# A decoder on one Trainium2 core: in cross attention, every third key tile is weighed as three bf16 products in place of one fp32 product

## Chip, cores and metric

The program runs on one core of a Trainium2 chip. The metric is the device time of one execution in microseconds (us); the median of several executions is given. The engines are TensorE (PE in the profile, with PEld for its weight loads), VectorE (DVE), ScalarE (ACT), GpSimd (POOL) and the DMA queues, here issued by SyncE (SP). Each engine works through its own list of instructions in order, and the engines meet only through semaphores.

## What is computed

Two decoder layers on x of shape (4, 256, 256) with a context of (4, 1601, 256). The part that the change touches is the cross attention of the second layer, for 16 query heads over 4 key/value heads of 128 channels:

```
q = rope(rms_norm(x @ Wq.T))            # (4, 16, 256, 128)
kv_in = concat([context, x], axis=1)    # 1601 + 256 = 1857 keys a batch row
k = rope(rms_norm(kv_in @ Wk.T));  v = kv_in @ Wv.T      # 4 heads, each used by 4 query heads
scores = q @ k.T / sqrt(128)
attn = softmax(scores) @ v
x = x + attn @ Wo.T
```

Everything is fp32 in the reference.

## The kernel before

The stages run one behind another: self attention, attention to the context as a memory, a ternary feed-forward, a gated scan, this cross attention, and the experts. The cross attention is `cross_stream` (L1385 on), by far the longest: its steps alone run from 704.0 to 1877.6 us.

**Groups, steps, slots.** A group g is one batch row with one key head: 16 groups (`GROUPS`). The 1857 keys of a group make `KT` = 15 tiles of 128 (the last has 65 rows), the 4 x 256 query columns make two halves of 512. So a group has `STEPS` = 30 steps: step j of a group is key tile t = j // 2 and half n = j % 2; a step counted through the whole stage is s = 30 g + j. The code of every engine is written as a loop over slots; in slot s each engine does its share for step s and whatever else is set down for that slot.

**One step.** `score` (PE, L1585) makes the scores as three bf16 products of high and low halves, 128 keys x 512 columns, in banks 0 and 1. `lower` (DVE, L1793) adds the column's negative bound and writes `lowered`, a ring of three. `exponent` (ACT, L1656) writes p into `p32`, a ring of four. `weigh` (PE, L1598) multiplies values by p in fp32 into bank 2 + n, over all 15 tiles; PE does it two slots late (`BEHIND` = 2). `accumulate` (POOL, L1733) adds p into `acc` for the sum of the softmax.

**Work for the next group in the same slots.** A unit (6 a group: two of queries, four chunks of keys and values) begins every 5 slots: `project` (PE, L1519), `square` and `take_values` (ACT, L1666, L1674), `rotate` and `vary` (DVE, L1825, L1828, L1835), `add_up` and `normalise` (POOL, L1738, L1743, L1748), `turn` (PE, L1561, a transposition into bank 6), `high` (ACT) and `low` (DVE, L1839). The bound of the next group's columns needs 32 coarse score products a group, one in most slots and two in slots 11 and 26: `piece` (PE, L1571) into bank 7, of which there is one, and `reduce_piece` (DVE, L1800). A piece waits until the piece before it has been reduced. `side` spreads the bound (PE L1609, DVE copy L1853, slots 27 and 28) through bank 6, and the output of the group before is projected through bank 6 too (L1622, DVE L1865, slots 7, 8, 12, 13).

**Order inside a slot.** PE: score(s), the first piece, weigh(s-2), project, other pieces, turn, side, output. DVE: lower(s), the pieces' reductions, att_low, low, rotate, vary, side, output. ACT: exponent(s), then squares, values, high. POOL: accumulate(s), add_up, normalise. These orders are written out by hand; no scheduler moves anything.

```
nc.tensor.matmul(ps[:, 2 + n, :], v[0:r, g % 2, t, :], p32[0:r, step % 4, :],
                 start=(t == 0), stop=(t == KT - 1)).then_inc(weighed, 1)
...
for slot in SLOTS:
    if 0 <= slot < ALL:
        lower(slot)
    for item in pieces_in(slot):
        reduce_piece(item)
```

Of the kernel before, what the change touches and what calls it, by code (L numbers as in the profile page):

```python
# [8 lines left out]
ALU = mybir.AluOpType  # L9
# [9 lines left out]
P = 128  # L19
BATCH, SEQ, DM = 4, 256, 256  # L20
QT = SEQ // P
# [11 lines left out]
class Stage:  # L33
# [14 lines left out]
    def sb(self, name, shape, dt=F32):  # L48
        return self.ctx.enter_context(self.nc.sbuf_tensor(f"{self.name}_{name}", shape, dt))
# [4 lines left out]
    def sem(self, name):  # L54
        s = self.ctx.enter_context(self.nc.semaphore(f"{self.name}_{name}"))
        self.numbers.append(s.num)
        return s
# [1093 lines left out]
def units_at(slot, late):  # L1151

    n, rest = divmod(slot - late + AHEAD, EVERY)
    return [n] if rest == 0 and 0 <= n < UNITS * GROUPS else []
# [230 lines left out]
def cross_stream(nc, x, const, a, w_q, w_kv, w_o, k_gain, q_gain, freq, ones, own, half, own_t, in_t, ctx_t,  # L1385
                 where, where_f, angle, turns, sin, k_tab, q_tab):

    with Stage(nc, "stream") as st:
# [2 lines left out]
        cos = angle  # L1391
        SCALE = float(HD) ** -0.5
        BEHIND = 2
        k_t = [sb(f"k_t_{part}", [P, 2, KT * P], BF16) for part in ("hi", "lo")]
        q_t = [sb(f"q_t_{part}", [P, 3, REP, SEQ], BF16) for part in ("hi", "lo")]
        v = sb("v", [P, 2, KT, HD])
# [11 lines left out]
        shift_all = sb("shift_all", [P, 2, QCOLS], BF16)  # L1408
        lowered = sb("lowered", [P, 3, HALF])
        p32 = sb("p32", [P, 4, HALF])  # L1410
        acc = sb("acc", [P, 2, QCOLS])
        inv = sb("inv", [P, REP * QT])
        att = [sb(f"att_{part}", [P, REP, SEQ], BF16) for part in ("hi", "lo")]
# [9 lines left out]
        where_loaded, pool_step, turns_ready, angle_step, angle_ready = (sem(s) for s in ("where_loaded", "pool_step", "turns_ready", "angle_step", "angle_ready"))  # L1423
        act_step, waves_ready, q_tab_ready, k_tab_ready = sem("act_step"), sem("waves_ready"), sem("q_tab_ready"), sem("k_tab_ready")
        dve_step = sem("dve_step")

        SLOTS = range(-AHEAD, ALL + 14)
        piece_at = {item: n for n, item in enumerate(item for s in SLOTS for item in pieces_in(s))}
# [62 lines left out]
        for s in SLOTS:  # L1491
            for items, n, step in (([("turn", u) for u in turns_in(s)], 0, 1), (sides_in(s), 1, 1), ([("out",) + o for o in outs_in(s)], 2, QT)):
                for item in items:
                    bank6_before[item] = tuple(past)
                    past[n] += step

        with nc.Block() as block:
            @block.sync
# [10 lines left out]
            def _(pe):  # L1509
# [79 lines left out]
                def weigh(step):  # L1589
                    g, j = divmod(step, STEPS)  # L1590
                    t, n = divmod(j, HALVES)
                    r = rows_of(t)
                    pe.wait_ge(p32_ready, step + 1)
                    if j == 0:
                        pe.wait_ge(v_taken, 2 * NCH * (g + 1))
                    if t == 0 and g >= 1:
                        pe.wait_ge(att_lo, HALVES * (g - 1) + n + 1)
                    nc.tensor.matmul(ps[:, 2 + n, :], v[0:r, g % 2, t, :], p32[0:r, step % 4, :],  # L1598
                                     start=(t == 0), stop=(t == KT - 1)).then_inc(weighed, 1)

                def side(item):
                    kind, g, n = item
# [44 lines left out]
            def _(ac):  # L1647
                wave_step = chain(ac, act_step)

                def exponent(step):  # L1650
                    r = rows_of(step % STEPS // HALVES)
                    ac.wait_ge(lowered_ready, step + 1)
                    if step >= 4:
                        ac.wait_ge(weighed, step - 3)
                        ac.wait_ge(acc_ready, step - 3)
                    nc.scalar.activation(p32[0:r, step % 4, :], lowered[0:r, step % 3, :], ACT.Exp, scale=SCALE).then_inc(p32_ready, 1)  # L1656

                def square(u, n):
                    ac.wait_ge(projected, part_at[(u, n)] + 1)
# [9 lines left out]
                def take_values(u, n):  # L1669
                    g, i, chunk = unit(u)  # L1670
                    tiles = tiles_of(chunk)[part_tiles(u, n)]
                    if g >= 2:
                        ac.wait_ge(weighed, STEPS * (g - 2) + HALVES * tiles.stop)
                    nc.scalar.copy(v[:, g % 2, tiles.start:tiles.stop, :], projected_values(u, n)).then_inc(v_taken, 1)  # L1674

                def high(u):
# [42 lines left out]
            def _(gp):  # L1719
# [20 lines left out]
                def normalise(u):  # L1740
# [5 lines left out]
                    if u >= 1:  # L1746
                        gp.wait_ge(turned, u)
                    nc.gpsimd.tensor_tensor(normed[:, 0:n], by_cos[:, u % 2, 0:n], bcast(rms[:, u % 2, 0:n], 2, HD),  # L1748
                                            ALU.mult).then_inc(normed_ready, 1)

                for slot in SLOTS:
                    if 0 <= slot < ALL:
                        accumulate(slot)
                    for u in units_at(slot, 6):
                        add_up(u)
                    for u in units_at(slot, 7):
                        normalise(u)
                    for b in range(1, BATCH):
# [21 lines left out]
            def _(ve):  # L1780
# [3 lines left out]
                def lower(step):  # L1784
                    g, j = divmod(step, STEPS)
                    t, n = divmod(j, HALVES)
                    r = rows_of(t)
                    if t == 0:
                        ve.wait_ge(side_taken, side_at[("spread", g, n)] + 1)
                    ve.wait_ge(scored, step + 1)  # L1790
                    if step >= 3:
                        ve.wait_ge(p32_ready, step - 2)
                    nc.vector.tensor_tensor(lowered[0:r, step % 3, :], ps[0:r, step % 2, :], shift_all[0:r, g % 2, n * HALF:(n + 1) * HALF],  # L1793
                                            ALU.add).then_inc(lowered_ready, 1)

                def reduce_piece(item):
                    g, m = item
# [70 lines left out]
                for slot in SLOTS:  # L1868
                    if 0 <= slot < ALL:
                        lower(slot)  # L1870
                    for item in pieces_in(slot):
                        reduce_piece(item)
                    g, late = divmod(slot, STEPS)
# [394 lines left out]
```

## Time and profile before

| | |
|---|---|
| median of 3 executions | 1992.65 us (1990.4 to 1993.88) |
| profiled execution, its own time | 1992.2 us |
| span of its trace | 1990.4 us |
| PE busy over the span | 1665.0 us (84%) |
| DVE busy | 1420.8 us (71%) |
| POOL busy | 1097.1 us (55%) |
| ACT busy | 732.3 us (37%) |
| steps of cross attention, first to last score | 704.0 to 1875.6 us |

The shares are means over stages that differ. For a change in one stage the busy times of that stage count, and within it the order of time: an engine that is busy 80% of a stage can still be late in single slots. Matmul records overlap (one of 512 columns is listed with 0.38 us but the next begins 0.216 us later), so prices of PE are taken from start to start; the same holds, less strongly, for DVE (0.69 us listed, 0.61 us to the next start). The span ends with the experts; nothing of this change touches them.

### The profile page before, as it was taken

The page shows a single profiled execution, that of the slowest core. Times are in us where ns is not written, and L with a number is a line of the kernel's source. Part 1 is how long each engine was busy: PE and PEld are TensorE (multiplying, and loading weights), DVE is VectorE, ACT ScalarE, POOL GpSimd, SP SyncE. Part 2 cuts the span into 40 slices and gives each one's busy share as a digit, 9 for nine tenths or more (in the row PEclk, how much of TensorE's full clock was granted, in tenths as well). Part 3 has the DMA queues.
Part 4 walks back from the last instruction along what each step waited for, and adds up shares of the span by engine and source line. Part 5 has one row for each costly group of instructions (what it writes and reads, how often), then busy time and mean ns, then how long its engine had stood idle before and what let it go on. Part 6 is the DMA issues. An engine that isn't in the chain of part 4 may idle for free. (4 is left out here: it accounts for less than half of the span.)

```text
span 1990.4 us, 25246 instructions
## 1 busy us (share of the span) xinstructions
PE 1665.0 (84%) x7962; PEld 954.4 (48%) x7962; DVE 1420.8 (71%) x2801; ACT 732.3 (37%) x1803; POOL 1097.1 (55%) x960
## 2 busy tenths in 40 slices
PE   3479889555643689999989999989999999999978
PEld 2368646423222335545545545545555555554444
DVE  7956411487768687787787887787787887886455
ACT  1344222121235244444335444335343443443342
POOL 4234200001204467887777797777797777776642
PEclk9789789868776899999999999999999999999879
DMA  1000160100004000000000000000000000000020
GB/s 58 1 1 1 53 212 0 43 0 20 8 2 176 1 1 1 1 34 1 1 1 1 1 34 1 1 1 1 0 1 1 1 1 1 1 1 1 1 65 22
DMA packets 27242, 37.37 MB, mean 19 GB/s; under 512 B 4572, under 2 KB 23780, under 8 KB 26856
## 3 DMA queue, kind: packets, MB, share of 16 engines
q1 hardware_dynamic: 27112, 35.76, 5.3%
q8 instruction: 66, 1.08, 0.2%
q14 instruction: 64, 0.52, 0.1%
HBM read 34.71 MB, written 1.05 MB: 18 GB/s over the span
## 5 line engine op out<-in xcount | busy, mean ns | idle before, releaser
L1733 POOL TENSOR_TENSOR stream_acc<-stream_acc,stream_p 128x512 f32<-128x512 f32 x448 | 570.0, 1275 | 212.9 <-ACT stream_p L1656 208.6
L1656 ACT ACTIVATE stream_p<-stream_lowered 128x512 f32<-128x512 f32 (+1 forms) x480 | 302.4, 630 | 678.5 <-DVE stream_lowered L1793 677.1
L1598 PE MATMUL stream_banks<-stream_p,stream_v 128*128 128x512 f32 (+1 forms) x960 | 490.0, 592 | 0.9 <-ACT stream_p L1656 0.9
L1793 DVE TENSOR_TENSOR stream_lowered<-stream_banks,stream_shift_all 128x512 f32<-128x512 f32 (+1 forms) x480 | 329.7, 687 | 187.0 <-PE stream_banks L1585 161.2
L1800 DVE TENSOR_REDUCE stream_tops<-stream_banks 128x1 f32<-128x512 f32 (+1 forms) x512 | 322.6, 630 | 35.2 <-PE stream_banks L1571 35.1
L1571 PE MATMUL stream_banks<-stream_k_t_hi,stream_q_t_hi 128*128 128x512 bf16 (+1 forms) x512 | 185.9, 363 | 33.4 <-DVE stream_tops L1800 31.4
L1598 PEld LDWEIGHTS stream_banks<-stream_p,stream_v 128*128 128x128 f32 (+1 forms) x960 | 175.3, 190 | 57.3 <-ACT stream_p L1656 2.7
L1585 PE MATMUL stream_banks<-stream_q_t_hi,stream_k_t_hi 128*128 128x512 bf16 (+1 forms) x480 | 182.8, 381 | 0.0
L1585 PE MATMUL stream_banks<-stream_q_t_lo,stream_k_t_hi 128*128 128x512 bf16 (+1 forms) x480 | 181.9, 379 | 0.0
L1585 PE MATMUL stream_banks<-stream_q_t_hi,stream_k_t_lo 128*128 128x512 bf16 (+1 forms) x480 | 181.9, 379 | 0.0
L1738 POOL TENSOR_TENSOR stream_by_cos<-stream_by_cos,stream_by_sin 128x512 f32<-128x512 f32 x96 | 120.2, 1252 | 50.6 <-DVE stream_by_sin L1828 50.3
L1571 PEld LDWEIGHTS stream_banks<-stream_k_t_hi,stream_q_t_hi 128*128 128x128 bf16 x512 | 49.9, 97 | 129.1 <-issue 85.4
L1748 POOL TENSOR_TENSOR stream_normed<-stream_by_cos,stream_rms 128x512 f32<-128x512 f32 x96 | 97.2, 1012 | 24.5 <-PE stream_banks L1561 17.3
L1666 ACT ACTIVATE stream_squares<-stream_banks 128x128 bf16<-128x128 f32 x368 | 95.2, 266 | 40.3 <-PE stream_banks L1519 40.3
L1743 POOL TENSOR_TENSOR stream_rms<-stream_var,cross_half 128x4 f32<-128x4 f32 x96 | 103.6, 1079 | 0.0
L1519 PEld LDWEIGHTS stream_banks<-cross_w_kv_hi,cross_in_t_hi 128*128 128x128 bf16 x416 | 40.6, 98 | 106.9 <-issue 97.8
L1561 PEld LDWEIGHTS stream_banks<-model_ident,stream_normed 128*128 128x128 f32 x368 | 43.2, 142 | 89.7 <-issue 60.8
L1561 PE MATMUL stream_banks<-model_ident,stream_normed 128*128 128x128 f32 x368 | 58.5, 281 | 32.2 <-DVE model_x L1865 25.6
L202 POOL TENSOR_TENSOR self_sm<-self_sm,self_mx 128x512 f32<-128x512 f32 (+1 forms) x32 | 46.9, 1466 | 63.1 <-DVE self_mx L288 63.1
L1519 PE MATMUL stream_banks<-cross_w_kv_hi,cross_in_t_hi 128*128 128x256 bf16 x416 | 79.6, 273 | 0.3 <-DVE stream_by_sin L1828 0.3
L1519 PE MATMUL stream_banks<-cross_w_kv_lo,cross_in_t_hi 128*128 128x256 bf16 x416 | 79.6, 273 | 0.0
L1519 PE MATMUL stream_banks<-cross_w_kv_hi,cross_in_t_lo 128*128 128x256 bf16 x416 | 79.5, 273 | 0.0
(387 smaller groups left out, 2991.1 us busy)
## 6 DMA issues: line engine op xcount, KB each, us to landing
memory_ctx_t<-in_ctx_t SPq DMA_DIRECT2D x4, 1601.0 KB
cross_ctx_t<-in_ctx_t SPq DMA_DIRECT2D x4, 1601.0 KB, 7.1
memory_ctx<-in_ctx SPq DMA_DIRECT2D x4, 1536.0 KB
cross_w_raw_q<-in_L_xattn_Wq SPq DMA_DIRECT2D x1, 2048.0 KB, 12.4
cross_w_raw_o<-in_L_xattn_Wo SPq DMA_DIRECT2D x1, 2048.0 KB, 19.6
moe_raw_up<-in_L_ffn_wi SPq DMA_DIRECT2D x8, 256.0 KB, 5.0
model_x<-in_x SPq DMA_DIRECT2D x1, 1024.0 KB, 5.1
ffn_raw_fc<-in_L_ffn_w_fc SPq DMA_DIRECT2D x1, 1024.0 KB, 5.0
```

Source lines behind the costliest of these rows:

```text
L1519: last = nc.tensor.matmul(out, rows, moving(two, c), start=(n == 0), stop=(n == 3 * DC - 1))
L1561: last = nc.tensor.transpose(ps[:, 6, h * P:(h + 1) * P], normed[:, h, :], const["ident"][:])
L1571: nc.tensor.matmul(ps[:, 7, 0:n], q_t[0][:, g % 3, h, q * P:(q + 1) * P], k_t[0][:, g % 2, s:s + n], start=True, stop=True).then_inc(piece ...
L1585: last = nc.tensor.matmul(ps[0:r, step % 2, :], k_t[one][:, g % 2, t * P:t * P + r], q_t[two][:, g % 3, 2 * n:2 * n + 2, :], start=(one == ...
L1598: nc.tensor.matmul(ps[:, 2 + n, :], v[0:r, g % 2, t, :], p32[0:r, step % 4, :], start=(t == 0), stop=(t == KT - 1)).then_inc(weighed, 1)
L1656: nc.scalar.activation(p32[0:r, step % 4, :], lowered[0:r, step % 3, :], ACT.Exp, scale=SCALE).then_inc(p32_ready, 1)
L1733: nc.gpsimd.tensor_tensor(acc[0:r, g % 2, cols], acc[0:r, g % 2, cols], p32[0:r, step % 4, :], ALU.add).then_inc(acc_ready, 1)
L1738: nc.gpsimd.tensor_tensor(by_cos[:, u % 2, 0:n], by_cos[:, u % 2, 0:n], by_sin[:, u % 2, 0:n], ALU.add).then_inc(summed, 1)
L1743: nc.gpsimd.tensor_tensor(rms[:, u % 2, 0:n], var[:, u % 2, 0:n], half[:, 0:n], ALU.pow).then_inc(rms_ready, 1)
L1748: nc.gpsimd.tensor_tensor(normed[:, 0:n], by_cos[:, u % 2, 0:n], bcast(rms[:, u % 2, 0:n], 2, HD), ALU.mult).then_inc(normed_ready, 1)
L1793: nc.vector.tensor_tensor(lowered[0:r, step % 3, :], ps[0:r, step % 2, :], shift_all[0:r, g % 2, n * HALF:(n + 1) * HALF], ALU.add).then_i ...
L1800: nc.vector.tensor_reduce(tops[:, i, c:c + 1], ps[:, 7, 0:CHUNKS[c][1]], AX_X, ALU.max).then_inc(piece_taken, 1)
```

## The change

Tiles 1, 4, 7, 10 and 13 of every group (`SPLIT`) are weighed as v_hi p_hi + v_lo p_hi + v_hi p_lo in bf16, the other ten tiles as before. That is 10 of 30 steps of a group (j = 2, 3, 8, 9, 14, 15, 20, 21, 26, 27), 160 of 480 steps in all. The halves are made on three engines: ACT casts p to bf16 right behind the exponential; DVE subtracts it from p (`p_rest`), one slot later, between `lower` and the reductions; ACT casts the tile's values and POOL subtracts (`values_rest`), behind `add_up`.

```
+        SPLIT = range(1, KT, 3)
+        p_part = [sb(f"p_part_{part}", [P, HALVES, HALF], BF16) for part in ("hi", "lo")]
+        v_part = [sb(f"v_part_{part}", [P, 2, len(SPLIT), HD], BF16) for part in ("hi", "lo")]
@@ weigh, PE
-                    nc.tensor.matmul(ps[:, 2 + n, :], v[0:r, g % 2, t, :], p32[0:r, step % 4, :],
-                                     start=(t == 0), stop=(t == KT - 1)).then_inc(weighed, 1)
+                    if t in SPLIT:
+                        pe.wait_ge(p_lo_ready, split_at[step] + 1)
+                        pe.wait_ge(v_lo_ready, len(SPLIT) * g + SPLIT.index(t) + 1)
+                        for one, two in ((0, 0), (1, 0), (0, 1)):
+                            last = nc.tensor.matmul(ps[:, 2 + n, :], v_part[one][:, g % 2, SPLIT.index(t), :], p_part[two][:, n, :],
+                                                    start=False, stop=False)
+                        last.then_inc(weighed, 1)
+                    else:
+                        nc.tensor.matmul(ps[:, 2 + n, :], v[0:r, g % 2, t, :], p32[0:r, step % 4, :],
+                                         start=(t == 0), stop=(t == KT - 1)).then_inc(weighed, 1)
@@ exponent, ACT
+                    if step in split_at:
+                        ac.wait_ge(p32_ready, step + 1)
+                        if split_before[step] is not None:
+                            ac.wait_ge(weighed, split_before[step] + 1)
+                        nc.scalar.copy(p_part[0][:, step % HALVES, :], p32[:, step % 4, :]).then_inc(p_hi_ready, 1)
@@ take_values, ACT
+                    for t in range(tiles.start, tiles.stop):
+                        if t in SPLIT:
+                            nc.scalar.copy(v_part[0][:, g % 2, SPLIT.index(t), :], projected_values(u, n)[:, t - tiles.start, :])
@@ POOL
+                def values_rest(u):
+                    gp.wait_ge(v_taken, keys_at[(u, 1)] + 1)
+                    for t in tiles_of(chunk):
+                        if t in SPLIT:
+                            nc.gpsimd.tensor_tensor(v_part[1][:, g % 2, SPLIT.index(t), :], v[:, g % 2, t, :],
+                                                    v_part[0][:, g % 2, SPLIT.index(t), :], ALU.subtract).then_inc(v_lo_ready, 1)
                     for u in units_at(slot, 6):
                         add_up(u)
+                        values_rest(u)
@@ DVE
+                def p_rest(step):
+                    ve.wait_ge(p_hi_ready, split_at[step] + 1)
+                    nc.vector.tensor_tensor(p_part[1][:, step % HALVES, :], p32[:, step % 4, :], p_part[0][:, step % HALVES, :],
+                                            ALU.subtract).then_inc(p_lo_ready, 1)
                     if 0 <= slot < ALL:
                         lower(slot)
+                    if slot - 1 in split_at:
+                        p_rest(slot - 1)
                     for item in pieces_in(slot):
                         reduce_piece(item)
```

What stands in a row on DVE in slots 27 and 28 of group 12, where the bound of the next group is spread (L1853): before,

```order
L1793 TENSOR_TENSOR stream_lowered<-stream_banks,stream_shift_all 128x512
L1800 TENSOR_REDUCE stream_tops<-stream_banks 128x1
L1853 CAST stream_shift_all<-stream_banks 128x512
L1793 TENSOR_TENSOR stream_lowered<-stream_banks,stream_shift_all 65x512
L1800 TENSOR_REDUCE stream_tops<-stream_banks 128x1
L1825 TENSOR_TENSOR stream_by_cos<-stream_banks,cross_k_tab_cos 128x256
L1828 TENSOR_TENSOR stream_by_sin<-stream_banks,cross_k_tab_sin 128x2x64 x2
L1853 CAST stream_shift_all<-stream_banks 128x512
```

and now, with the new line numbers:

```order
L1827 TENSOR_TENSOR stream_lowered<-stream_banks,stream_shift_all 128x512
L1832 TENSOR_TENSOR stream_p_part_lo<-stream_p,stream_p_part_hi 128x512
L1839 TENSOR_REDUCE stream_tops<-stream_banks 128x1
L1892 CAST stream_shift_all<-stream_banks 128x512
L1827 TENSOR_TENSOR stream_lowered<-stream_banks,stream_shift_all 65x512
L1832 TENSOR_TENSOR stream_p_part_lo<-stream_p,stream_p_part_hi 128x512
L1839 TENSOR_REDUCE stream_tops<-stream_banks 128x1
L1864 TENSOR_TENSOR stream_by_cos<-stream_banks,cross_k_tab_cos 128x256
L1867 TENSOR_TENSOR stream_by_sin<-stream_banks,cross_k_tab_sin 128x2x64 x2
L1892 CAST stream_shift_all<-stream_banks 128x512
```

In both slots a subtraction of two SBUF tiles (L1832) now stands ahead of the reduction and of everything behind it.

On POOL, the work of two units of keys in a row: before,

```order
L1738 TENSOR_TENSOR stream_by_cos<-stream_by_cos,stream_by_sin 128x512
L1733 TENSOR_TENSOR stream_acc<-stream_acc,stream_p 128x512
L1743 TENSOR_TENSOR stream_rms<-stream_var,cross_half 128x4
L1748 TENSOR_TENSOR stream_normed<-stream_by_cos,stream_rms 128x512
L1733 TENSOR_TENSOR stream_acc<-stream_acc,stream_p 128x512 x4
```

and now,

```order
L1761 TENSOR_TENSOR stream_by_cos<-stream_by_cos,stream_by_sin 128x512
L1781 TENSOR_TENSOR stream_v_part_lo<-stream_v,stream_v_part_hi 128x128
L1756 TENSOR_TENSOR stream_acc<-stream_acc,stream_p 128x512
L1766 TENSOR_TENSOR stream_rms<-stream_var,cross_half 128x4
L1771 TENSOR_TENSOR stream_normed<-stream_by_cos,stream_rms 128x512
L1756 TENSOR_TENSOR stream_acc<-stream_acc,stream_p 128x512 x4
```

The values' subtraction (one in a chunk, two in the second chunk of keys) comes ahead of the accumulation and of `normed`, for which PE's transposition waits.

## Rows read from the trace of the kernel before

**Rows 1.** Busy time by stretch: steps, group 12, group 15 (us, instructions).

```profile
core 0: us, PE busy (x) PEld busy (x) DVE busy (x) ACT busy (x) POOL busy (x), PEclk, DMA share, GB/s
704.00:1877.60 1173.60, 1127.04 (x5385) 599.52 (x5382) 932.11 (x1842) 494.64 (x1389) 906.08 (x802) 1.00 0.01 4
1618.21:1692.99 74.78, 72.67 (x359) 39.54 (x356) 59.31 (x121) 30.51 (x94) 55.23 (x48) 1.00 0.00 1
1827.47:1877.60 50.13, 50.11 (x193) 24.63 (x191) 25.44 (x43) 20.23 (x33) 36.71 (x31) 1.00 0.00 1
```

**Rows 2.** Timeline of PE, slot 21: start us, us, what.

```profile
1670.94 0.38 PE L1585 MATMUL stream_banks<-stream_q_t_hi,stream_k_t_hi 128*128 128x512 bf16 x1
1671.15 0.38 PE L1585 MATMUL stream_banks<-stream_q_t_lo,stream_k_t_hi 128*128 128x512 bf16 x1
...
1671.72 1.02 PE L1598 MATMUL stream_banks<-stream_p,stream_v 128*128 128x512 f32 x2
1672.58 0.38 PE L1519 MATMUL stream_banks<-cross_w_kv_hi,cross_in_t_hi 128*128 128x256 bf16 x2
```

**Rows 3.** Groups of instructions: DVE and ACT operations on SBUF tiles, POOL subtraction.

```profile
L266 DVE TENSOR_TENSOR self_gained<-self_rot,self_ln_g 128x512 f32<-128x512 f32 x8 | 5.5, 684 | 0.0
L2075 ACT CAST moe_inner_hi<-moe_inner 128x512 bf16<-128x512 f32 x16 | 9.5, 615 | 1.2 <-DVE moe_inner L2007 1.2
L1970 POOL TENSOR_TENSOR moe_w_up_lo<-moe_raw_up,moe_w_up_hi 128x512 bf16<-128x512 f32 x8 | 9.1, 1164 | 21.3 <-ACT moe_w_down_hi L2051 21.3
L1210 POOL TENSOR_TENSOR cross_q_tab_cos<-cross_angle,cross_q_gain 128x128 f32<-128x128 f32 x8 | 4.4, 544 | 13.4 <-ACT cross_angle L1234 13.4
```

**Rows 4.** Timelines of DVE and POOL where both have SBUF inputs.

```profile
719.34 1.91 DVE L1900 SCALAR_TENSOR_TENSOR cross_angle<-cross_turns,cross_angle 128x960 f32<-128x960 f32 x1
718.97 1.27 POOL L1733 TENSOR_TENSOR stream_acc<-stream_acc,stream_p 128x512 f32<-128x512 f32 x1 [0.34 <-ACT stream_p L1656]
849.58 1.66 DVE L1906 TENSOR_TENSOR cross_in_t_lo<-cross_ctx_t,cross_in_t_hi 128x1024 bf16<-128x1024 f32 x1
850.12 2.00 POOL L1743 TENSOR_TENSOR stream_rms<-stream_var,cross_half 128x4 f32<-128x4 f32 x1
```

**Rows 5.** Who waited for whom, in total: us, times, longest.

```profile
PE stream_banks L1571 <- DVE stream_tops L1800: 31.4, 53, 1.9
PEld stream_banks L1561 <- POOL stream_normed L1748: 27.6, 46, 2.2
```

**Rows 6.** Timelines of DVE, POOL and PE, slots 27 to 29 of group 12.

```profile
1686.60 0.67 DVE L1793 TENSOR_TENSOR stream_lowered<-stream_banks,stream_shift_all 128x512 f32<-128x512 f32 x1
1690.91 0.69 DVE L1853 CAST stream_shift_all<-stream_banks 128x512 bf16<-128x512 f32 x1
1686.50 1.27 POOL L1738 TENSOR_TENSOR stream_by_cos<-stream_by_cos,stream_by_sin 128x512 f32<-128x512 f32 x1 [0.74 <-DVE stream_by_sin L1828]
1688.01 1.27 POOL L1733 TENSOR_TENSOR stream_acc<-stream_acc,stream_p 128x512 f32<-128x512 f32 x1 [0.25 <-ACT stream_p L1656]
1692.55 0.60 PE L1561 MATMUL stream_banks<-model_ident,stream_normed 128*128 128x128 f32 x4
```

**Rows 7.** Timelines of DVE, POOL and PE, slots 22 to 24 of group 12.

```profile
1674.42 0.68 DVE L1793 TENSOR_TENSOR stream_lowered<-stream_banks,stream_shift_all 128x512 f32<-128x512 f32 x1
1674.44 1.27 POOL L1738 TENSOR_TENSOR stream_by_cos<-stream_by_cos,stream_by_sin 128x512 f32<-128x512 f32 x1
1678.16 1.04 POOL L1748 TENSOR_TENSOR stream_normed<-stream_by_cos,stream_rms 128x512 f32<-128x512 f32 x1
1676.18 0.30 PE L1571 MATMUL stream_banks<-stream_k_t_hi,stream_q_t_hi 128*128 128x321 bf16 x1
1679.47 0.60 PE L1561 MATMUL stream_banks<-model_ident,stream_normed 128*128 128x128 f32 x4
```

**Rows 8.** Timelines of DVE and PE, slots 9 and 10 of group 12.

```profile
1643.05 0.67 DVE L1793 TENSOR_TENSOR stream_lowered<-stream_banks,stream_shift_all 128x512 f32<-128x512 f32 x1
1643.65 0.68 DVE L1800 TENSOR_REDUCE stream_tops<-stream_banks 128x1 f32<-128x512 f32 x1
1644.47 0.38 PE L1571 MATMUL stream_banks<-stream_k_t_hi,stream_q_t_hi 128*128 128x512 bf16 x1
```

More of the change, by code:

```diff
@@ L1425, in cross_stream @@
         dve_step = sem("dve_step")
+        p_hi_ready, p_lo_ready, v_lo_ready = sem("p_hi_ready"), sem("p_lo_ready"), sem("v_lo_ready")
         SLOTS = range(-AHEAD, ALL + 14)
@@ L1495, in cross_stream @@
                     past[n] += step
+        split_at = {step: n for n, step in enumerate(step for step in range(ALL) if step % STEPS // HALVES in SPLIT)}
+        split_before = {step: last for last, step in zip([None] * HALVES + list(split_at), split_at)}
         with nc.Block() as block:
@@ L1749, in normalise @@
                                             ALU.mult).then_inc(normed_ready, 1)
+                def values_rest(u):
+                    g, i, chunk = unit(u)
+                    if i < QT:
+                        return
+                    gp.wait_ge(v_taken, keys_at[(u, 1)] + 1)
[3 more added lines that the diff above has]
+                                                    v_part[0][:, g % 2, SPLIT.index(t), :], ALU.subtract).then_inc(v_lo_ready, 1)
                 for slot in SLOTS:
```

## The prediction

> **What bounds the kernel now.** I read the busy times by stretch first. Over the steps of cross attention, 704.0 to 1877.6 us, PE is busy 1127 of 1173.6 us, DVE 932, POOL 906, ACT 495, at a granted clock of 1.00, and DMA does next to nothing [rows 1]. So PE bounds the stage on average: in group 12 it idles 2.1 us of 74.78, while DVE idles 15.5 [rows 1]. A saving on PE is worth its full size only where nobody is late behind it. So the second view is the list of waits: PE already waits for the reduction of the piece before (31.4 us, 53 times) and for POOL's `normed` (27.6 us, 46 times) [rows 5]. These are doors through which DVE and POOL reach PE, and the change puts work on both. The third view is the timeline of one group, where one sees how far each door is from closing.
>
> **What PE saves.** A fp32 product starts at 1671.72 and the next instruction at 1672.58: 0.86 us. Three bf16 products of the same columns cost three times the distance from 1670.94 to 1671.15, 0.216 us with the decimals averaged over a slot: 0.65 us [rows 2]. Their weight loads lie under the matmul before, as those of the scores do. Saved: 0.21 us a split step, 2.1 us a group of ten, 160 x 0.21 = 33 us in all. This is the change's whole gain; all else is price.
>
> **What ACT pays.** 160 casts of p at about 0.62 us, the nearest row being a cast of an SBUF tile of this size [rows 3], and some 80 small ones: 100 us and 20 us on an engine that is busy 495 of 1173.6 [rows 1]. ACT's cast is behind an exponential that DVE's `lower` releases, and `p_rest` comes a slot later, so I cost it at nothing; what hides it is ACT's own idle time of some 1.3 us a slot. Behind it are queued the squares and values, for which `rotate` waits one slot later. If that cover failed, it would cost up to 0.6 us at slots 2 and 27.
>
> **What POOL pays.** 80 subtractions of 128x128. A quarter of the 512-wide subtraction of 1.16 us is 0.29, the 128x128 product took 0.54 [rows 3]; I take 0.4. Five a group make 2 us, in front of `normed`.
>
> **What DVE pays.** 160 subtractions of two SBUF tiles of 512 columns. Such a one took 0.68 us without company [rows 3]; from start to start DVE operations of this width keep 0.60 to 0.61 (1643.05 to 1643.65 [rows 8]). Ten a group: 6.1 us of the 15.5 idle. But they aren't without company. In the trace, DVE's two-input operation at 719.34 took 1.91 us: POOL's accumulation had started at 718.97 and ended at 720.24, and DVE ended 1.01 us behind that. The other way round, DVE's subtraction from 849.58 to 851.24 is followed by a POOL operation which took 2.00 us in place of 1.02 [rows 4]. So when POOL works, `p_rest` first waits for the end of its operation, and then POOL's next waits for `p_rest`. The price of one is thus 0.61 us at least and 0.61 + 1.27 at most. `lower`, the reductions and `rotate` read PSUM and don't show this.
>
> The Trainium skill says the same, "SBUF — State Buffer", section on who interferes with whom: a DVE instruction with two SBUF inputs contends with a GpSimd instruction that reads SBUF, and whoever is first keeps the shared pair for the whole instruction. The trace agrees, with 1.91 and 2.00 us. By that rule the sum is the one below; without it every `p_rest` would cost 0.61 us, which leads towards the first rival.
>
> **Where it lands, place by place**, in group 12, with 0.2 us from a reduction's end to the piece on PE (the tightest distance in the trace: the reduction of 1643.65 is through at 1644.26, the piece starts at 1644.47 [rows 8]).
>
> *Slots 27 to 29.* `lower`(27) is through at 1687.21, but POOL's operation from 1686.50 lasts to 1687.77 [rows 6]. `p_rest`(26) runs from there to 1688.38, the reduction to 1689.0, the spread's copy to 1689.6, `lower`(28) to 1690.2. POOL's accumulation was put off by `p_rest` and ends at 1689.7; its next operation, of 1.0 us, is then in `p_rest`(27)'s way to 1690.7. Then `p_rest` to 1691.3, reduction to 1691.9, rotation 0.85 us to 1692.75: the copy that started at 1690.91 starts 1.8 us later. Bank 6 is free for the transposition only behind it (0.6 + 0.2); that gives 1693.55 in place of 1692.55 [rows 6]. Net +1.0 us; the 0.4 us that PE saved here are gone in it.
>
> *Slots 21 to 24.* `lower`(22) starts at 1674.42, some 0.2 later now; POOL's addition of 1674.44 lasts to 1675.71. `p_rest`(21) runs to 1676.3, the reduction (0.4 for 321 columns) to 1676.7, so the piece of 1676.18 goes at 1676.9: +0.7. POOL then has `values_rest` 0.4 and was put off 0.6, so `normed` ends near 1680.1 in place of 1679.2, and the transposition of 1679.47 goes at about 1680.2 [rows 7]. Net +0.7.
>
> *Slots 9 to 11.* DVE is the one PE waits for already: the piece of 1644.47 is 0.2 behind the reduction. `p_rest`(8) delays both by 0.6, and `p_rest`(9) meets POOL and holds the second piece of slot 11 [rows 8]. PE saves 0.4 behind the first of them. Net +0.3.
>
> *Slots 3 to 5 and 15 to 17.* The pattern is that of slots 9 to 11 with more room in front (0.7 to 1.0 us) and two or three short waits for POOL. I take the same +0.3 for each, an estimate between -0.4 (all hidden) and +0.7.
>
> Sum: 1.0 + 0.7 + 0.3 + 0.3 + 0.3 = +2.6 us a group, in place of -2.1. Groups 14 and 15 are different: in the last, PE is busy 50.11 of 50.13 us, DVE 25, POOL 36.7 [rows 1]; there `p_rest` comes close to its product, since slots last only 1.7 us. I take nothing for both, between -4 and +4. Total 14 x 2.6 = +36 us. On the profiled execution's own 1992.2 us (1.8 over its span, 0.4 below the median) this gives **2028.6 us**.
>
> **Rivals.**
>
> *The doors stay open* (faster). If POOL's phases fall elsewhere, and the waits for it are short, `p_rest` costs 0.61 and only slots 9 to 11 and 27 to 29 close. That is a gross loss near 1.0 us a group against 2.1 saved: 14 x -1.1 less 4 at the end, 1973; with everything hidden, 1992 - 33 = 1959. For it: DVE has 15.5 us of idle time a group. Against it: `p_rest` stands ahead of the reduction, which has 0.2 to 1.0 us of room before the next piece. It decides where a `p_rest` takes less than that room. Chance 0.22.
>
> *It comes out even* (within 0.2%, about what a measurement of this kernel can tell from no change, 4 us). Stalls of 2.1 a group meet savings of 2.1: 1988 to 1996. Chance 0.08.
>
> *DVE becomes the bound* (slower still). Every `p_rest` meets POOL at a full 0.6 and `vary`, `p_rest` and POOL hold each other up in turn, so that nothing of PE's saving is seen: stalls of 4.7 a group come net of no saving, 14 x 4.7 = 66, 2058. For it: POOL is busy 74% of group 12 and would be over 80%. Against: DVE still sums to 59.3 + 6.1 + 3 = 68 of 77 us. Chance 0.15.
>
> *It does not do what it says*: the three products don't run at 0.216 us each, because weight loads of `v_part` show. The scores' loads don't show in the same pattern, so this is within the 0.03 that I leave; each 0.1 us on a product would add 48 us.
>
> **The numbers.** Forecast (2000 to 2045) 0.52, open doors 0.22, even 0.08, DVE bound 0.15, products 0.03. Slower by over 0.2%: 0.52 + 0.15 + 0.03 = 0.70; same 0.08; faster 0.22. The range holds the forecast, evenness, the upper rival's middle and the milder half of the first: 1975 to 2062.
>
> **What would show it.** Right: `p_rest` of 160, mean 0.85 to 1.1 us with a floor of 0.68; L1571's wait for `tops` over 60 us from 31; the transposition waiting longer for the spread copy; the split product at 0.65 us; group 12 at 77 us; DVE busy near 1050 us. Wrong: a mean of `p_rest` below 0.75, PE idle in group 12 still 2 us and the group at 72.7, or PE waiting at the product itself for `p_part_lo`, which I take to be ready 1 us ahead in the full groups.

## The result and the profile after

| | before | changed |
|---|---|---|
| median | 1993.27 us | 2042.87 us (2040.24 to 2046.36, 4 executions) |
| ratio | | 1.0252, 95% interval 1.0233 to 1.0271 |
| profiled execution, its own time and span | 1992.2, 1990.4 us | 2043.5, 2041.4 us |

The change costs 50 us. The forecast was 2028.6 us, 36 above the kernel before; 2042.9 lies at the upper end of its main case, 2000 to 2045.

First the busy times by stretch, for the steps and for group 12, with the columns of [rows 1]:

```profile
704.80:1928.00 1223.20, 1118.93 (x5546) 584.49 (x5544) 1046.26 (x2002) 603.72 (x1620) 958.23 (x875) 0.99 0.01 4
1661.40:1737.50 76.10, 71.74 (x369) 38.39 (x367) 65.64 (x132) 37.34 (x108) 58.45 (x54) 1.00 0.00 1
```

Over the steps PE is busy 1119 us instead of 1127, in 1223 us instead of 1174; DVE went up by 114 us, ACT by 109, POOL by 52. PE's share fell from 96% to 91%: it no longer bounds the stage alone. Group 12 takes 76.1 us instead of 74.8.

The groups of instructions that answer to [rows 3] (the subtraction on DVE and the cast on ACT) can now be measured; before, they were estimated from neighbours:

```profile
L1832 DVE TENSOR_TENSOR stream_p_part_lo<-stream_p,stream_p_part_hi 128x512 bf16<-128x512 f32 x160 | 140.0, 875 | 8.0 <-ACT stream_p_part_hi L1676 8.0
L1676 ACT CAST stream_p_part_hi<-stream_p 128x512 bf16<-128x512 f32 x160 | 98.9, 618 | 5.1
L1578 PE MATMUL stream_banks<-stream_k_t_hi,stream_q_t_hi 128*128 128x512 bf16 (+1 forms) x512 | 186.7, 365 | 86.7 <-DVE stream_tops L1839 82.2
```

The line of one instruction, with the shortest, median and longest duration in ns, shows how uneven the subtraction is, and the values' subtraction on POOL:

```profile
L1832 DVE TENSOR_TENSOR stream_p_part_lo<-stream_p,stream_p_part_hi x160: 672/724/1459, 712.8 to 1925.2; 128x512 bf16<-128x512 f32 x160
...
L1781 POOL TENSOR_TENSOR stream_v_part_lo<-stream_v,stream_v_part_hi x80: 418/428/887, 645.9 to 1832.6; 128x128 bf16<-128x128 f32 x80
```

And the waits, as [rows 5]:

```profile
PE stream_banks L1578 <- DVE stream_tops L1839: 82.2, 129, 3.7
PEld stream_banks L1568 <- POOL stream_normed L1771: 32.9, 48, 2.2
```

PE's wait for the reduction rose from 31 to 82 us, that for `normed` only from 28 to 33.

The timelines of DVE, POOL and PE in slots 27 to 29 of group 12 answer to [rows 6]:

```profile
1730.70 0.67 DVE L1827 TENSOR_TENSOR stream_lowered<-stream_banks,stream_shift_all 128x512 f32<-128x512 f32 x1
1731.30 1.11 DVE L1832 TENSOR_TENSOR stream_p_part_lo<-stream_p,stream_p_part_hi 128x512 bf16<-128x512 f32 x1
1732.33 0.68 DVE L1839 TENSOR_REDUCE stream_tops<-stream_banks 128x1 f32<-128x512 f32 x1
...
1734.13 0.72 DVE L1832 TENSOR_TENSOR stream_p_part_lo<-stream_p,stream_p_part_hi 128x512 bf16<-128x512 f32 x1
...
1736.10 0.67 DVE L1892 CAST stream_shift_all<-stream_banks 128x512 bf16<-128x512 f32 x1
...
1730.59 1.27 POOL L1761 TENSOR_TENSOR stream_by_cos<-stream_by_cos,stream_by_sin 128x512 f32<-128x512 f32 x1 [0.74 <-DVE stream_by_sin L1867]
1734.27 1.46 POOL L1766 TENSOR_TENSOR stream_rms<-stream_var,cross_half 128x4 f32<-128x4 f32 x1
...
1733.15 0.38 PE L1578 MATMUL stream_banks<-stream_k_t_hi,stream_q_t_hi 128*128 128x512 bf16 x1 [0.24 <-DVE stream_tops L1839]
1733.37 0.38 PE L1609 MATMUL stream_banks<-stream_p_part_hi,stream_v_part_hi 128*128 128x512 bf16 x1
1733.59 0.38 PE L1609 MATMUL stream_banks<-stream_p_part_hi,stream_v_part_lo 128*128 128x512 bf16 x1
1733.80 0.38 PE L1609 MATMUL stream_banks<-stream_p_part_lo,stream_v_part_hi 128*128 128x512 bf16 x1
...
1737.03 0.63 PE L1568 MATMUL stream_banks<-model_ident,stream_normed 128*128 128x128 f32 x4 [0.24 <-POOL stream_normed L1771]
```

Four things are to be seen. The first subtraction starts at 1731.30, waits for POOL's operation of 1730.59 to end at 1731.86, and takes 1.11 us. The second finds POOL nearly done and takes 0.72; POOL's next operation then takes 1.46 us instead of 1.02. The piece on PE goes 0.2 us behind the reduction. And the three products start 0.22 apart, as the forecast priced them.

### The profile page after: what moved, and what is told of

Same layout as the page of the kernel before. It is cut to its first block and busy times, and to the rows that moved or that the text cites. A ratio compares the mean times of both kernels' runs of the same rounds, so it can differ in the third digit from the quotient of the medians.

```text
span 2041.4 us, 26376 instructions
## 1 busy us (share of the span) xinstructions
PE 1662.0 (81%) x8122; PEld 943.9 (46%) x8122; DVE 1536.1 (75%) x2961; ACT 842.8 (41%) x2043; POOL 1151.6 (56%) x1040
## 3 DMA queue, kind: packets, MB, share of 16 engines
q8 instruction: 68, 1.11, 0.2%
## 5 line engine op out<-in xcount | busy, mean ns | idle before, releaser
L1613 PE MATMUL stream_banks<-stream_p,stream_v 128*128 128x512 f32 (+1 forms) x640 | 326.7, 592 | 0.0
L1832 DVE TENSOR_TENSOR stream_p_part_lo<-stream_p,stream_p_part_hi 128x512 bf16<-128x512 f32 x160 | 140.0, 875 | 8.0 <-ACT stream_p_part_hi L1676 8.0
L1613 PEld LDWEIGHTS stream_banks<-stream_p,stream_v 128*128 128x128 f32 (+1 forms) x640 | 116.4, 190 | 35.5 <-ACT stream_p L1671 0.9
L1766 POOL TENSOR_TENSOR stream_rms<-stream_var,cross_half 128x4 f32<-128x4 f32 x96 | 110.3, 1149 | 0.0
L1676 ACT CAST stream_p_part_hi<-stream_p 128x512 bf16<-128x512 f32 x160 | 98.9, 618 | 5.1
L1526 PEld LDWEIGHTS stream_banks<-cross_w_kv_hi,cross_in_t_hi 128*128 128x128 bf16 x416 | 40.8, 98 | 88.7 <-issue 66.5
L1526 PE MATMUL stream_banks<-cross_w_kv_hi,cross_in_t_hi 128*128 128x256 bf16 x416 | 80.1, 274 | 0.3 <-DVE stream_by_sin L1867 0.3
```

The lines of the kernel that those rows point to most:

```text
L1526: last = nc.tensor.matmul(out, rows, moving(two, c), start=(n == 0), stop=(n == 3 * DC - 1))
L1766: nc.gpsimd.tensor_tensor(rms[:, u % 2, 0:n], var[:, u % 2, 0:n], half[:, 0:n], ALU.pow).then_inc(rms_ready, 1)
L1832: nc.vector.tensor_tensor(p_part[1][:, step % HALVES, :], p32[:, step % 4, :], p_part[0][:, step % HALVES, :], ALU.subtract).then_inc(p_lo ...
```

## The experiments

All are edits of the changed kernel. Ratios are to the kernel before on the same chip (1990.5 to 1993.3 us); "us" is (ratio - 1) x 1992.

| kernel | median us | ratio (95%) | us |
|---|---|---|---|
| changed | 2042.9 | 1.0252 (1.0233 to 1.0271) | +50 |
| fp32 products, all else kept | 2058.8 | 1.0336 (1.0318 to 1.0353) | +67 |
| subtraction behind the reductions | 2040.1 | 1.0237 (1.0219 to 1.0255) | +47 |
| no subtraction on POOL | 2036.8 | 1.0237 (1.0220 to 1.0254) | +47 |
| one SBUF input in its place | 2014.0 | 1.0108 (1.0091 to 1.0125) | +22 |
| subtraction half as wide | 2013.2 | 1.0097 (1.0077 to 1.0117) | +19 |
| one input, and behind | 2004.8 | 1.0075 (1.0058 to 1.0091) | +15 |
| tiles 2, 5, 8, 11, behind | 2005.0 | 1.0075 (1.0059 to 1.0092) | +15 |
| tiles 8, 11, both subtractions behind | 1994.5 | 1.0010 (1.0000 to 1.0019) | +2 |
| no subtraction on DVE | 1978.7 | 0.9935 (0.9919 to 0.9952) | -13 |
| neither subtraction | 1975.6 | 0.9924 (0.9908 to 0.9941) | -15 |
| products alone | 1972.1 | 0.9889 (0.9870 to 0.9908) | -22 |
| two products, no subtraction on DVE | 1967.2 | 0.9867 (0.9848 to 0.9886) | -26 |

### Which part of the change costs

**No subtraction on DVE.**

```
-                    if slot - 1 in split_at:
-                        p_rest(slot - 1)
...
-                        pe.wait_ge(p_lo_ready, split_at[step] + 1)
+                        pe.wait_ge(p_hi_ready, split_at[step] + 1)
```

> The changed kernel without its 160 subtractions on DVE (L1832): the low half of p is filled once with zeros and never written again, so its part of the third product is left out of the result; products, casts and the subtraction of the values stand as in the changed kernel, and PE waits for ACT's cast instead. Theory A (the subtraction on DVE, ahead of the reductions, with its waits for POOL, is the whole price): PE's saving of 33 us shows nearly in full, 1955 to 1968 us, and L1571/L1578's wait for the reduction falls back to 25 to 35 us. Rival B (the values' subtraction on POOL delays normed and the transposition): 1990 to 2015, with the wait for normed still above 27 us. Rival C (the three products or ACT's casts cost what they seem to save): above 2025.

It took 1978.7 us, 63 less than the changed kernel, and the wait for the reduction fell back to 30 us. So the DVE subtraction is the price. But only 13 of PE's 33 us came out, and the time lies in none of the three ranges; theory A has the cause right and the gain too high. The wait for `normed` was 48 us here:

```profile
PEld stream_banks L1569 <- POOL stream_normed L1773: 48.0, 49, 2.2
PE stream_banks L1579 <- DVE stream_tops L1841: 30.3, 51, 2.0
```

**fp32 products with everything else in place.**

```
-                        for one, two in ((0, 0), (1, 0), (0, 1)):
-                            last = nc.tensor.matmul(ps[:, 2 + n, :], v_part[one][...], p_part[two][:, n, :], ...)
-                        last.then_inc(weighed, 1)
+                        nc.tensor.matmul(ps[:, 2 + n, :], v[0:r, g % 2, t, :], p32[0:r, step % 4, :],
+                                         start=False, stop=False).then_inc(weighed, 1)
```

> The changed kernel with all products in fp32 as before, but with every cast, subtraction and wait of the change in place (the halves are made and not used). Theory A: the stalls stay and PE's saving is gone; where PE waits for a reduction the saving was lost already, so less than 33 us come on top: 2050 to 2072 us. If the products had saved nothing (rival C), it stays at 2043, within 4 us.

2058.8 us, as theory A expected: within the changed kernel the bf16 products are worth 17 us of the 33 that they save on PE. That excludes rival C.

**Neither subtraction**, and then **the products alone**, without ACT's casts of p:

```
-                        values_rest(u)
...
-                        nc.scalar.copy(p_part[0][:, step % HALVES, :], p32[:, step % 4, :]).then_inc(p_hi_ready, 1)
```

> The changed kernel with neither subtraction (both low halves are zeros filled once; what they add is left out of the result); the three products and ACT's casts stay. Theory: what stood between 1978.7 (no DVE subtraction) and PE's full saving of 33 us is the values' subtraction on POOL: 1959 to 1967 us. If it stays at 1975 to 1980, the rest lies with ACT's casts or with PE's own waits for DVE, which no saving of PE shortens.

> Only the change on PE is left: three bf16 products in ten steps of a group, on tiles whose high and low halves of p are zeros filled once (the split tiles' share is left out of the result); no cast of p on ACT, no subtraction on DVE or POOL. With ACT's casts in place it was 1975.6 us, 15 below the kernel before and not 33. If ACT's casts of p take the rest: 1957 to 1965. If PE's saving is lost at waits for POOL's normed and for DVE that PE cannot shorten: 1973 to 1978, with the wait for normed above 35 us, from 27.6 before.

They took 1975.6 and 1972.1 us, 15 and 22 below the kernel before by their ratios; the intervals of the two just touch, at 0.991. The first is the second case of its expectation, not the 1959 to 1967 of its theory: the values' subtraction is worth about 2 us once the DVE one is gone, within the noise. ACT's casts of p are worth at most the 7 us between the two ratios, and the traces say less: from the first `lower` to the last the two kernels differ by 2.4 us, and another 3 lie ahead of the first step, where no p is cast in either. What repeats is in groups 0, 4 and 8, which save 0.2 us each with the casts and 0.85 without; a group like 12 saves 1.7 us with or without them. With nothing but the products and the small casts of the values left, the last third of the saving is still missing. In that kernel PE waits for others more than before (27.6 and 31.4 us):

```profile
PEld stream_banks L1569 <- POOL stream_normed L1767: 36.8, 46, 2.1
PE stream_banks L1579 <- DVE stream_tops L1835: 32.6, 57, 2.0
```

Nine us of the missing eleven stand in the first row: PE arrives earlier and `normed` does not. The second expectation asked for this row above 35 us, and it is, though the time came out between its two cases.

**No subtraction on POOL, the DVE one in place.**

> The changed kernel without its 80 subtractions on GpSimd (the values' low halves are zeros filled once, so that part of the second product is left out); the DVE subtraction stays. POOL's share was seen in the kernel without the DVE subtraction: slot 24 of a group became 0.5 us longer there, since normed came 0.4 us later. If the two prices lie on the same doors, this run gains little on the changed kernel's 2042.9: 2033 to 2041 us. If they add: 2025 to 2033.

2036.8 us, the first case: 6 us less than the changed kernel by the medians, 3 by the ratios, whose intervals overlap. The two prices lie largely on the same waits.

### Length, company or place

**One SBUF input.** The same width and place, but without the second SBUF input.

```
-                    nc.vector.tensor_tensor(p_part[1][:, step % HALVES, :], p32[:, step % 4, :], p_part[0][:, step % HALVES, :],
-                                            ALU.subtract).then_inc(p_lo_ready, 1)
+                    nc.vector.tensor_reduce(p_part[1][:, step % HALVES, :], p32[:, step % 4, :].rearrange("p (n o) -> p n o", o=1), AX_X,
+                                            ALU.max).then_inc(p_lo_ready, 1)
```

> The changed kernel with the DVE subtraction replaced by a reduction over an axis of one element, which reads one SBUF tile and writes the same bf16 tile (the low half is then p itself rounded, so the result is a different one). Same width, same place, one SBUF input in place of two. If the waiting for POOL matters as forecast: the operation shows 0.68 us flat from 0.875 mean, DVE loses 30 us of busy time, POOL's normed comes earlier, and the time falls to 2012 to 2028 us. If the waiting for POOL is harmless and only the place and the 0.6 us count: 2038 to 2043.

2014.0 us. The operation is flat, as the line of its instruction shows beside the uneven one above:

```profile
L1832 DVE TENSOR_REDUCE stream_p_part_lo<-stream_p x160: 662/674/687, 712.4 to 1894.4; 128x512 bf16<-128x512 f32 x160
```

The time is in the range expected if the waiting matters: waiting for POOL, and POOL's waiting in turn, are worth 29 us. Place, width and output tile stayed the same. The number of SBUF inputs and the kind of instruction changed together, and no run takes these two apart. The Trainium skill, "SBUF — State Buffer", section on who interferes with whom, says that a two-input `tensor_tensor` contends with GpSimd's reads and a `tensor_reduce` never does. The trace agrees: the longest of each takes 1459 ns against 687.

**Half as wide.**

```
-                    nc.vector.tensor_tensor(p_part[1][:, step % HALVES, :], p32[:, step % 4, :], p_part[0][:, step % HALVES, :],
+                    nc.vector.tensor_tensor(p_part[1][:, step % HALVES, 0:HALF // 2], p32[:, step % 4, 0:HALF // 2], p_part[0][:, step % HALVES, 0:HALF // 2],
```

> The changed kernel with the DVE subtraction over the first 256 of 512 columns (the other half's low part is zeros filled once and left out of the result): about 0.41 us listed in place of 0.68 when alone, at the same place, and still with two SBUF inputs. If the price goes by the time that DVE spends (64 us for 0.875 us each): half to 0.7 of it remains, 2010 to 2023. If the wait for POOL's operation in progress, which does not get shorter, is the larger part: 2026 to 2036.

2013.2 us, in the lower of the two ranges. The group's mean fell from 875 to 640 ns:

```profile
L1834 DVE TENSOR_TENSOR stream_p_part_lo<-stream_p,stream_p_part_hi 128x256 bf16<-128x256 f32 x160 | 102.4, 640 | 8.0 <-ACT stream_p_part_hi L1676 8.0
```

Put side by side: 102 us of this work on DVE cost 32 us (+19 against -13 without any), 108 us of the one-input form cost 35, and the full 140 us cost 63. The first hundred microseconds cost a third of their length, the last 32 to 38 most of theirs (28 to 31). That the one-input form and the half-wide one, which still waits for POOL, lie on one curve suggests that POOL's share acts mostly through the time that it adds to DVE; three kernels are few for a curve, and this is not shown.

**Behind the reductions.**

```
-                    if slot - 1 in split_at:
-                        p_rest(slot - 1)
                     for item in pieces_in(slot):
                         reduce_piece(item)
+                    if slot - 1 in split_at:
+                        p_rest(slot - 1)
```

> The changed kernel with one edit: the subtraction stands behind the slot's reductions and not ahead of them. Theory A in its strict form (the door is the reduction that the next piece waits for): the wait of the piece for the reduction falls from 82 to some 35 us and the time to 1985 to 2010 us; the product two slots on still has its low half in time. Rival D (DVE is simply late over several slots, wherever the subtraction stands, through the spread copy, the rotation and lower): above 2025, with the waits moved to the transposition or to the products.

2040.1 us, against 2042.9; the intervals of the two ratios overlap. Theory A in its strict form is wrong, and rival D came about. The wait for the reduction did fall, from 82 to 34 us, and others took its place, `normed` above all:

```profile
PEld stream_banks L1568 <- POOL stream_normed L1771: 59.2, 52, 2.2
PE stream_banks L1578 <- DVE stream_tops L1839: 33.7, 54, 1.4
PE stream_banks L1568 <- POOL stream_normed L1771: 24.5, 35, 2.0
...
PE stream_banks L1609 <- DVE stream_p_part_lo L1832: 13.4, 41, 1.1
```

The two rows of `normed` are 84 us here and 41 in the changed kernel. The reduction was where PE met the lateness, not what made it. A plain group such as 12 is even 0.3 us slower this way (+1.63 against +1.35).

**Both edits together.**

> The changed kernel with both edits: the DVE operation reads one SBUF tile (a reduction over an axis of one element, so the low half is p itself rounded) and stands behind the slot's reductions. Alone they gave 2014.0 and 2040.1 us. If the place mattered only as long as the operation doesn't wait for POOL, the two together give more than their sum: 1985 to 2003 us. If the place hardly counts at all: 2008 to 2014.

2004.8 us: 6.6 us below the one-input form by the ratios, whose intervals just touch, where the place alone gave 3. The place seems to count a little once the operation has stopped meeting POOL. It fell between the two cases expected.

### Is there a share that pays

**Other tiles.** Slots 27 and 28 stay free of it.

```
-        SPLIT = range(1, KT, 3)
+        SPLIT = range(2, KT - 1, 3)
```

> The changed kernel with the subtraction behind the reductions and other tiles split: 2, 5, 8 and 11, four in place of five. PE saves 128 x 0.21 = 27 us. The subtractions fall into slots 5, 6, 11, 12, 17, 18, 23, 24 of a group, where DVE had 0.8, 0.5, 1.45, 0.8, 1.1, 0.0, 0.9 and 0.0 us of idle time before, and slots 27 and 28 (the spread copy) stay free. Theory: the price is set by the slots in which the subtraction meets a full DVE or a working POOL: 1985 to 2010 us. If it goes by their number alone (50 us / 160 each, as in the changed kernel): 2033.

2005.0 us, +15, with 27 us saved on PE; the time lies within what was expected and on the slow side. 128 subtractions cost 42 us in all, 0.33 each; in the changed kernel 160 cost 83 (50 and the 33 saved), 0.52 each. The mean duration is the same (861 ns). Part of the difference can be the smaller number, since the first subtractions cost less than the last (above).

The starts of `lower` in the trace say more than the total. Groups 3, 7 and 11 to 13 are 0.7 us faster than in the kernel before, where five tiles behind the reductions made them 1.3 to 1.6 us slower. The 2.0 to 2.3 us between them exceed the 1.7 us that two subtractions of mean length take, so the place seems to count as well; one subtraction of values and two casts fewer stand in the difference too, and no run separates them. Groups 1, 5 and 9 are 0.3 us faster; 0, 4, 8 and 2, 6, 10 lose 1.6 to 2.8 us each, the last two 1.1 and 1.7. Four tiles thus pay in eight of the sixteen groups. Splitting only there was not tried.

**Two tiles.** Tiles 8 and 11, with both subtractions behind what PE waits for.

```
+        SPLIT = range(8, KT - 1, 3)
...
                     for u in units_at(slot, 7):
                         normalise(u)
+                        values_rest(u)
```

> Only tiles 8 and 11 are split, the subtraction of p stands behind the reductions, and that of the values behind normed on POOL. PE saves 64 x 0.21 = 13 us. If a split pays wherever DVE has idle time in its slot and nothing is put ahead of normed: 1978 to 1986. If the saving is lost at the transposition of slot 24 and the last two groups pay for POOL: 1989 to 1995, no gain.

1994.5 us, ratio 1.0010: no gain, the second case. The 13 us saved on PE are spent again. No version with the same products and a low half of p beat the kernel before.

**Two products.**

```
-                        for one, two in ((0, 0), (1, 0), (0, 1)):
+                        for one, two in ((0, 0), (1, 0)):
```

> The kernel without the DVE subtraction (1978.7 us), and without the third product, which it made with a low half of zeros: p enters the split tiles rounded to bf16, the values as high and low half. The rest of p is left out of the result. PE has 160 x 0.216 = 34.6 us less to do. If PE is still the bound: 1944 to 1952. If the saving goes the way of the first, with under half of it seen: 1960 to 1970.

1967.2 us, the fastest of all, and faster than both kernels by 1.3% and 3.8%; but it drops the rest of p in a third of the tiles, so it isn't the same arithmetic. As a test of the bound: 35 us less on PE gave 13, and the waits for `normed` went up to 67.3 and 20.2 us, from 48.0 and 12.8. The expected case of under half of it seen is right. The wait for the reduction rose less, from 30.3 to 40.8 us, so what ends these groups is more often POOL's chain than PE; that is read from the waits, and no run shortened POOL's chain.

## Why the forecast was right, and what it missed

**The prices held.** The subtraction on DVE: 0.85 to 1.1 us forecast with a floor of 0.68, measured 0.875 with a shortest of 0.672. The product 0.65 us, measured three starts of 0.22. The wait of the piece over 60 us, measured 82. DVE busy near 1050 us, measured 1046. POOL's values 0.4 us, measured 0.43 by the median (0.58 by the mean). That the loss is DVE's and that POOL makes it worse is shown by the runs: 63 us for the subtraction, 29 of them gone with the one-input form.

One of the signs did not come: the transposition does not wait longer for the spread copy (1.6 us in all before, 1.2 now). In slot 28 of group 12 the copy starts 1.1 us later, counted from `lower` in slot 27, but the transposition of 1737.03 is released by `normed` (rows above).

**The sum of group 12 was too high.** Forecast +2.6 us, measured 76.13 less 74.78 = +1.35, from its first `lower` to that of group 13:

```profile
1662.27 0.69 DVE L1827 TENSOR_TENSOR stream_lowered<-stream_banks,stream_shift_all 128x512 f32<-128x512 f32 x1 [0.43 <-issue]
1738.40 0.69 DVE L1827 TENSOR_TENSOR stream_lowered<-stream_banks,stream_shift_all 128x512 f32<-128x512 f32 x1 [0.43 <-issue]
```

By the starts of `lower` in both traces, slots 9 to 11 cost +0.3 (forecast +0.3), slots 21 to 24 +0.5 (+0.7), slots 27 to 29 +0.4 (+1.0), slots 3 to 5 +0.1 and 15 to 17 nothing (+0.3 each). In slots 27 and 28 the path through the copy and bank 6 was not the one that held, and the second wait was wrong: the text let POOL's next operation start ahead of `p_rest`(27), and it was the other way round, 0.72 us on DVE and 1.46 on POOL (rows above).

**"14 x 2.6" is the step that failed.** It took group 12 for every group. Groups 3, 7 and 11 to 13 are like it and cost 6.5 us in all, where the sum has 13.0. Groups 1, 2, 5, 6, 9 and 10 cost 19.9 against 15.6, and groups 0, 4 and 8 cost 18.7 against 7.8: group 4 takes 84.9 us from `lower` to `lower`, 80.1 before, and group 0 costs 7.6. Together 45 us against 36. A good part of what is missing is in the sentence that costed ACT's casts at nothing, covered by 1.3 us of idle time a slot, or at 0.6 us where that cover failed. In groups 0, 4 and 8 the cover is not there: ACT makes the sines of the next row's tables. The timelines of ACT, DVE and PE in group 4:

```profile
1063.14 1.28 ACT L1232 ACT_TABLE_LOAD   x1
...
1067.47 1.28 ACT L1671 ACT_TABLE_LOAD   x1
1068.77 0.63 ACT L1671 ACTIVATE stream_p<-stream_lowered 128x512 f32<-128x512 f32 x1
1069.43 0.62 ACT L1676 CAST stream_p_part_hi<-stream_p 128x512 bf16<-128x512 f32 x1
...
1070.08 1.21 DVE L1832 TENSOR_TENSOR stream_p_part_lo<-stream_p,stream_p_part_hi 128x512 bf16<-128x512 f32 x1 [2.24 <-ACT stream_p_part_hi L1676]
...
1072.04 0.38 PE L1578 MATMUL stream_banks<-stream_k_t_hi,stream_q_t_hi 128*128 128x512 bf16 x1 [2.47 <-DVE stream_tops L1839]
```

For 5.6 us (1063.14 to 1068.77) ACT does no exponential. It did none before either: POOL waited 4.6 us for it, and DVE 1.5 us at the low half of the queries. But PE ran on, since the reduction stood ahead of that wait, and DVE's next `lower` asks only for the exponential three steps back. Now DVE stands 2.24 us at `p_rest`, with the reduction and `lower` queued behind it, and PE waits 2.47 us for that reduction. The group of L1832 sums DVE's waits to 8.0 us, in three places. So the change added a wait, DVE's for ACT, which the forecast named and then costed by the average slot.

Two of the runs bear this out. The one-input form is never held up by POOL but has the same three waits of 8.0 us: there group 12 costs nothing (0.03 us), while groups 4 and 8 still cost 3.15 each and group 0 4.7. Without the DVE subtraction groups 4 and 8 cost 0.06 us. No run took the sines away.

In group 5 DVE is late through the two-input subtraction of the context that was there already (0.84 us in the same place before):

```profile
1163.37 1.31 DVE L1832 TENSOR_TENSOR stream_p_part_lo<-stream_p,stream_p_part_hi 128x512 bf16<-128x512 f32 x1
...
1165.01 1.73 DVE L1947 TENSOR_TENSOR cross_in_t_lo<-cross_ctx_t,cross_in_t_hi 128x512 bf16<-128x512 f32 x1
1166.66 0.68 DVE L1827 TENSOR_TENSOR stream_lowered<-stream_banks,stream_shift_all 128x512 f32<-128x512 f32 x1
```

Two such operations behind one another each wait for an operation of POOL.

**The last groups** cost +2.1 and +1.9 us where nothing was taken for both, 4.0 together, at the edge of the -4 to +4 kept.

So the forecast is right in its direction and in its cause, and that its total is near is partly luck, by two errors against each other: plain groups cost half of what was summed, groups 0, 4 and 8 twice to three times as much. The second error is the larger, and the sum came out 14 us too low. The doors as such were the wrong picture in one respect: moving the subtraction out of the way of the reduction gained nothing that is measured. What stays open is how the loss in groups 1, 2, 5, 6, 9 and 10 (2.5 to 4.6 us each) divides between the tables on POOL and the context on DVE; no run took these apart.

## What to carry to other kernels

A saving on the busiest engine is worth what its neighbours let through: here 22 of 33 us with hardly any added work, 17 with all of it. Added work on an engine with idle time cost a third of its length at first here and most of it later, so price the last microseconds, not the first; and look through the whole trace for places where the covering engine is away, not at one typical group. When a wait in the list is long, moving the work that it names may only rename the wait.

## What the runs showed of the hardware

In the changed kernel's trace, 46 of the 160 two-input subtractions (128x512) start while GpSimd does nothing and take 0.67 to 0.68 us. One that starts while a 128x512 operation of GpSimd still has more than about 0.1 us to go ends 0.54 to 0.56 us behind that operation, and so takes up to 1459 ns. The one-input reduction in the same place takes 662 to 687 ns.

The size of the operation that waits does not matter, and one SBUF input does not always protect. DVE's `tensor_scalar` of 128x4, in the kernel before, takes 154 ns alone; in 58 of 96 cases it starts inside GpSimd's accumulation and ends 0.02 to 0.03 us behind it, up to 1217 ns:

```profile
L1835 DVE TENSOR_SCALAR stream_var<-stream_ss x96: 154/677/1217, 638.6 to 1784.7; 128x4 f32<-128x4 f32 x80, 128x3 f32<-128x3 f32 x16
```

What GpSimd is doing does matter. Its `rms` of 128x4 takes 1.02 us and was put off to 1.46 by one subtraction. But 17 subtractions started while `rms` was under way, 0.64 us or more after its start, and took 0.67 to 0.68 us, as alone. So that whoever is first keeps the pair for the whole instruction, as the prediction has it, is borne out for GpSimd's operations of 128x512 and not for this one.
